# Mamba layer and mixture of experts on one core: scatters, a weight remainder and a norm re-ordered at the seam between scan and expert tiles

## The reference

```
x: 8 sequences x 512 tokens x 256 channels
x = layernorm(x + mamba(x))      # in_proj, conv of 4 taps, silu, softplus, a scan over time
                                 # with 16 states per channel, gate, out_proj, inner layernorm
x = layernorm(x + ffn(x))        # 8 experts, 4 of them per token by router logits:
    gate, up = x @ gate_up[e].T  # 256 -> 2 x 512
    act = (min(up,7)+1 ...) * silu-like(gate)
    out = act @ down[e].T        # 512 -> 256, weighted by a softmax over the 4 chosen
```

## Time and profile before

| | |
|---|---|
| median of 3 runs | 1254.55 us (1253.52 to 1254.76) |
| profiled execution | 1253.93 us, its span 1252.1 us |
| PE busy | 1144.7 us, 91% |
| DVE busy | 1043.4 us, 83% |
| ACT busy | 872.8 us, 70% |
| POOL busy | 759.1 us, 61% |
| mean granted TensorE clock | 0.959 |

### The profile page before, as it was taken

One profiled execution on the slowest core, in us unless ns is written; L12 is line 12 of the kernel. 1 busy time (PEld: TensorE's weight loads), 2 busy tenths in 40 slices (PEclk: granted clock), 3 DMA queues, 4 the chain that ended last, 5 costly groups with the idle time before them and its releaser, 6 DMA issues. The chain is left out here.

```text
span 1252.1 us, 17793 instructions
## 1 busy us (share of the span) xinstructions
PE 1144.7 (91%) x5150; PEld 795.0 (63%) x5150; DVE 1043.4 (83%) x1797; ACT 872.8 (70%) x1553; POOL 759.1 (61%) x535
## 2 busy tenths in 40 slices
PE   9889998999999997688999999999999999999950
PEld 4334353535343443257888888888888888888850
DVE  4999999999999999978876777777777777777744
ACT  4685959595969696625776777677777677677745
POOL 0456659888888887986764544454445544454453
PEclk9899999999999998898999999999999999999985
DMA  2643444646364645555796666656666566665638
GB/s 95 232 171 137 137 180 151 214 162 226 146 231 152 222 166 192 190 194 194 221 296 174 147 170 164 170 133 162 170 159 163 136 172 171 160 143 154 170 40 275
DMA packets 69263, 217.27 MB, mean 174 GB/s; under 512 B 7520, under 2 KB 43232, under 8 KB 56288
## 3 DMA queue, kind: packets, MB, share of 16 engines
q1 hardware_dynamic: 33888, 171.63, 37.4%
q0 software_dynamic: 26880, 36.72, 17.8%
q10 hardware_dynamic: 8448, 8.39, 2.0%
HBM read 165.55 MB, written 51.15 MB: 173 GB/s over the span
## 5 line engine op out<-in xcount | busy, mean ns | idle before, releaser
L1155 DVE TENSOR_TENSOR_SCAN state<-decay,p_bu 128x512 f32<-128x512 f32 x256 | 297.1, 1201 | 1.4 <-ACT decay L897 1.4
L697 PE MATMUL p_y<-read,small 128*128 128x512 f32 x512 | 252.6, 633 | 40.7 <-POOL read L1347 40.6
L1663 POOL DMA_INDIRECT total<-o_v,tok x136 | 252.8, 1859 | 37.5 <-issue 36.9
L697 PEld LDWEIGHTS p_y<-read,small 128*128 128x128 f32 x512 | 100.0, 201 | 178.6 <-issue 108.2
L1661 POOL TENSOR_TENSOR scrap<-neg_half 128x1 f32<-128x1 f32 x36 | 22.8, 633 | 271.6 <-ACT o_v L1579 259.2
L534 ACT ACTIVATE gate_v<-p_g,bias 128x512 f32<-128x512 f32 x144 | 98.7, 686 | 118.4 <-PE p_up L524 114.2
L542 DVE TENSOR_SCALAR up_v<-up_v 128x512 f32<-128x512 f32 x144 | 69.6, 483 | 129.7 <-ACT up_v L537 128.8
L897 ACT ACTIVATE decay<-dt,scan_rate 128x511 f32<-128x511 f32 x256 | 162.3, 709 | 10.6 <-DVE state L1155 10.0
L1347 POOL TENSOR_TENSOR read<-state,bc 128x1024 f32<-128x1024 f32 x64 | 127.6, 2000 | 27.8 <-DVE p_bu L1146 13.5
L555 ACT ACTIVATE ah<-a_v 128x512 fp32r<-128x512 f32 x144 | 91.5, 635 | 58.8 <-DVE a_v L548 58.8
L1389 POOL DMA_INDIRECT queues<-rows,index x112 | 115.5, 1031 | 26.8 <-issue 24.9
(11 more groups left out here) (247 smaller groups left out, 2984.6 us busy)
## 6 DMA issues: line engine op xcount, KB each, us to landing
bc<-bc_rows SPq DMA_DIRECT2D x32, 1024.0 KB, 4.8
first_raw<-in_w_experts SPq DMA_DIRECT2D x19, 1668.0 KB, 7.0
raw_w<-in_w_experts SPq DMA_DIRECT2D x18, 1668.0 KB, 7.1
first_wh<-bc_rows SPq DMA_DIRECT2D x16, 1024.0 KB, 4.7
first_wl<-bc_rows SPq DMA_DIRECT2D x16, 1024.0 KB, 5.0
first_rows<-queues SPq DMA_DIRECT2D x19, 544.0 KB, 3.6
xq<-queues SPq DMA_DIRECT2D x18, 544.0 KB, 3.7
queues<-pad SPq DMA_DIRECT2D x9, 544.0 KB, 6.2
```

Of the source, the lines that this page charges most:

```text
L697: mm = pe.matmul(p_y[h][:, :], ident[:, :], read[:, t % 4, h, :], start=False, stop=(t == SLOTS - 1))
L1155: dve.tensor_tensor_scan(state[t % 4][:, h, :], decay[(SLOTS * s.n + t) % AHEAD][:, h, :], p_bu[:, h * LEN:(h + 1) * LEN], 0.0, ALU.mult, ...
L1663: pool.indirect_dma_start(total, bass.IndirectOffsetOnAxis(ap=tokens_of(t)[:, a:a + 1], axis=0), output_of(t)[:, a, :], None, compute_op=A ...
```

## The change

It concerns the end of stage 1 and the first two tiles. (1) Sequence 5's seven scatters leave round 7: `SCATTERS` now applies only in rounds that also prepare a sequence, and all 16 stand in round 8, three ahead of the first power, one ahead of the second, three ahead of the third, nine behind. (2) Tile 0's three weight remainders move from behind the gate to ahead of it, with a wait for the reads that use the buffer they overwrite. (3) `last_norm1` works on each output bank by itself as it becomes full, so that there are three powers in place of two. (4) TensorE transposes tile 0's rows one slot later, sequence 7's rows between the chunks 2 and 3 of tile 0, and tile 1's rows behind the routing. (5) VectorE computes the remainder of tile 0's first product ahead of the last ranking, and the first remainder of tile 1's weights behind the last count.

```
@@ pe_stage1
                 if r.like == SEQS and t == 0:
                     transpose_rows(r, 0)
                     transpose_rows(r, 1)
+                if r.like == SEQS and t == 1:
                     pe.wait_ge(s_bu, halves_done(r.s, -1))
                     transpose_tile(pe, Seq(0, 0))
...
-                if r.d and t == 0 and r.like != SEQS:
+                if r.d and t == 0 and r.like < SEQS:
                     transpose_rows(r, 0)
                     transpose_rows(r, 1)
-                if r.last and t == 0:
-                    transpose_tile(pe, Seq(0, 1))
                 if r.d and t == 1:
                     route(r)
+                if r.last and t == 1:
+                    transpose_tile(pe, Seq(0, 1))
...
                         up_projection(pe, Seq(0, 0), i)
+                        if i == 2:
+                            transpose_rows(ROUNDS[-1], 0)
+                            transpose_rows(ROUNDS[-1], 1)
@@ dve_stage1
-        def last_moments(which, source):
+        def last_moments(k, which, some, source):
...
         def last_norm1(r):
-            banks = [full(dve, r, f"o{b}") for b in range(2)]
...
+            half = TT // 2
+            for b in range(2):
+                bank, done = full(dve, r, f"o{b}")
+                some = range(half * b, half * (b + 1))
+                last_moments(b, 0, some, lambda t: bank[:, t % 2 * D:(t % 2 + 1) * D])
+                for t in some:
+                    last = dve.scalar_tensor_tensor(z[:, t, :], bank[:, t % 2 * D:(t % 2 + 1) * D], last_neg[:, 0, t:t + 1],
+                                                    ln_g[:, :], ALU.add, ALU.mult)
+                last.then_inc(done, 1)
             for b in range(2):
                 bank, n = r.block(f"o{b}")
                 dve.wait_ge(bank_read[bank], n)
...
+                dve.wait_ge(s_last_rstd, b + 1)
+                for t in range(half * b, half * (b + 1)):
+                    last = dve.scalar_tensor_tensor(z[:, t, :], z[:, t, :], rstd[:, 0, t:t + 1], x[:, t, :], ALU.mult, ALU.add)
             last.then_inc(s_last_z, 1)
...
+                if r.like == SEQS and t == 2:
+                    dve.wait_ge(s_read, SLOTS * (SEQS - 1) + 4 * (RING - 1))
+                    for i in range(3):
+                        rest_of_weights(dve, early, i)
                 if r.c and t == 2:
                     gate(r)
-                if r.like == SEQS and t == 2:
-                    for i in range(3):
-                        rest_of_weights(dve, early, i)
...
-                    rest_of_weights(dve, second, 0)
+                if r.last and t == 2:
+                    rest_of_product(dve, early, 0)
...
                 if r.last and t == 3:
-                    rest_of_product(dve, early, 0)
...
                     rest_of_product(dve, early, 1)
+                    rest_of_weights(dve, second, 0)
                     rest_of_weights(dve, second, 1)
@@ pool_stage1
-        NEXT_TO_LAST = {8: (0, 1, 2), 10: (3,), 11: (4, 5), 12: (6,)}
...
-                scatters = NEXT_TO_LAST if r.like == SEQS - 1 else SCATTERS
-                if r.d and r.b and t in scatters:
-                    scatter(r.s.at(-2), scatters[t])
+                if r.d and r.a and t in SCATTERS:
+                    scatter(r.s.at(-2), SCATTERS[t])
...
                 if r.like == SEQS and t == 0:
-                    scatter(r.s.at(-3), range(7, 14))
-                    last_power(0)
-                    scatter(r.s.at(-3), range(14, TT * TOPK))
-                    last_power(1)
+                    scatter(r.s.at(-3), range(0, 3))
+                    last_power(0, 0, slice(0, TT // 2))
+                    scatter(r.s.at(-3), range(3, 4))
+                    last_power(1, 0, slice(TT // 2, TT))
+                    scatter(r.s.at(-3), range(4, 7))
+                    last_power(2, 1, slice(0, TT))
+                    scatter(r.s.at(-3), range(7, TT * TOPK))
```

More of the change, by code:

```diff
@@ L1173, in residual @@
             last.then_inc(s_residual, 1)
-        def last_moments(which, source):
-            for t in range(TT):
+        def last_moments(k, which, some, source):
+            for t in some:
                 last = dve.bn_stats(last_stats[:, t, :], source(t))
             last.then_inc(s_last_stats, 1)
-            dve.wait_ge(s_last_stats, which + 1)
-            for t in range(TT):
+            dve.wait_ge(s_last_stats, k + 1)
+            for t in some:
                 last = dve.bn_aggr(last_mv[:, which, t, :], last_stats[:, t, :])
@@ L1183, in last_moments @@
             last.then_inc(s_last_mv, 1)
[L1184 to L1187, removed]
-        def last_norm1(r):
-            banks = [full(dve, r, f"o{b}") for b in range(2)]
[L1193 to L1201, removed]
+            dve.wait_ge(s_last_mv, k + 1)
@@ new lines, in last_moments @@
+            cols = slice(some[0], some[-1] + 1)
+            dve.tensor_scalar(last_mv[:, which, cols, 1], last_mv[:, which, cols, 1], EPS, None, ALU.add)
+            dve.tensor_scalar(last_neg[:, which, cols], last_mv[:, which, cols, 0], -1.0, None, ALU.mult)\
+               .then_inc(s_last_eps, 1)
+            dve.wait_ge(s_last_eps, k + 1)
+        def last_norm1(r):
+            half = TT // 2
[3 more added lines that the diff above has]
+                last_moments(b, 0, some, lambda t: bank[:, t % 2 * D:(t % 2 + 1) * D])
+                for t in some:
+                    last = dve.scalar_tensor_tensor(z[:, t, :], bank[:, t % 2 * D:(t % 2 + 1) * D], last_neg[:, 0, t:t + 1],
+                                                    ln_g[:, :], ALU.add, ALU.mult)
+                last.then_inc(done, 1)
@@ L1204, in last_norm1 @@
                 dve.wait_ge(bank_read[bank], n)
-            dve.wait_ge(s_last_rstd, 1)
-            for t in range(TT):
-                last = dve.scalar_tensor_tensor(z[:, t, :], z[:, t, :], rstd[:, 0, t:t + 1], x[:, t, :], ALU.mult, ALU.add)
+                dve.wait_ge(s_last_rstd, b + 1)
+                for t in range(half * b, half * (b + 1)):
+                    last = dve.scalar_tensor_tensor(z[:, t, :], z[:, t, :], rstd[:, 0, t:t + 1], x[:, t, :], ALU.mult, ALU.add)
             last.then_inc(s_last_z, 1)
@@ L1213, in last_norm2 @@
             dve.wait_ge(s_last_z, 1)
-            last_moments(1, lambda t: z[:, t, :])
+            last_moments(2, 1, range(TT), lambda t: z[:, t, :])
             dve.tensor_copy(rows_of_seq(s)[:, :, COL_TOKEN].bitcast(I32), token[:, TT * s.n:TT * (s.n + 1)])
-            dve.wait_ge(s_last_rstd, 2)
+            dve.wait_ge(s_last_rstd, 3)
             for t in range(TT):
@@ L1362, in power, with last_power @@
                 .then_inc(s_rstd, 1)
-        def last_power(which):
-            pool.wait_ge(s_last_eps, which + 1)
-            pool.tensor_tensor(rstd[:, which, :], last_mv[:, which, :, 1], neg_half[:, :], ALU.pow).then_inc(s_last_rstd, 1)
+        def last_power(k, which, some):
+            pool.wait_ge(s_last_eps, k + 1)
+            pool.tensor_tensor(rstd[:, which, some], last_mv[:, which, some, 1], neg_half[:, some], ALU.pow)\
+                .then_inc(s_last_rstd, 1)
         def scale(r):
```

## The result

The changed kernel takes 1266.11 us (median of 4 executions, 1264.29 to 1266.57) against 1254.03 for the kernel before, measured beside it: ratio 1.0093, 95% interval 1.0079 to 1.0107. That is 12.1 us slower. The forecast was 7.6 slower, and its range ended at 1264.5. The profiled execution took 1266.57 us with a span of 1264.7, 12.6 above the span before. In both traces the last scan ends within 0.06 us of the same time, so rows of the two can be set side by side directly. Columns are as in the rows of before.

What follows compares the result with a forecast made beforehand. The prediction took GpSimd's chain of scatters and adds, reaching TensorE's tile loop through tile 4's token copy, as the bound. 1253.93 + 7.8 (chain) - 0.2 (tile 5) = 1261.5 us; range 1256.5 to 1264.5.

Steps and rivals of the forecast that it cites:

- The lock: Seam: VectorE's L498 and GpSimd's read 15 and offset exclude each other for whole instructions; gate at 551.8, 0.7 us later.
- the chain of scatters: GpSimd, seam: seven moved scatters at 1.27 us each, 8.9 us, stand in front of sequence 6.
- tile 4's token copy: VectorE, L578: waits 8 us or more for tile 2's adds, near 662; before, its wait measured 0.26 us.
- the half-clock start of tile 5: TensorE, tile 5: after 9 us without work it starts at half clock, costing 1.8 to 2.5 us.
- the vanished wait for rows: TensorE, behind tile 5's chunk 0: the 2.20 us wait for the next tile's rows goes.
- Rival A: Seam: no exclusion, reads slip through; gate at 548.4, chain +4.5 us, 1258.2 us; chance 0.14.
- B: Rival, GpSimd's chain: all 7.56 us of idle swallow the new work; 1252.9 us, no change; chance 0.10.
- C: Rival: GpSimd's chain does not bind, the seam's gain carries; faster, 1249.8 us; chance 0.08.
- D: Rival: slow scatters stay slow, or more collisions with tile 1's moved remainder; 1263.3 us; chance 0.08.
- the chain's shift: GpSimd: sequence 6's scatters start at 579.4 instead of 571.55, +7.8 us, passed on to tile 4's token copy.
- Nothing behind 571.55 can absorb it: GpSimd behind sequence 6's old start: the two idle spells, 2.23 and 2.93 us, are the chain's own; +7.8 us passes on.
- The -0.2 for tile 5: TensorE, tile 5: half-clock start (1.8 to 2.5 us) against the vanished 2.20 us wait for rows, net -0.2.

Runs made afterwards that it cites:

- the run with own tokens: The changed kernel with a token buffer of its own for tile 4, the wait for tile 2's adds moved in front of its read_output: 1.0037, median 1258.3 us.
- the gap filled: The changed kernel with six products of constants that nobody reads on TensorE between sequence 6's routing and project_out: 1.0067 of the kernel before, median 1263.13 us.
- the pads early: The changed kernel with SyncE's eight pad writes moved from tile 4's turn to tiles 2 and 3, four each: 1.0021 of the kernel before, median 1256.48 us.

## What the prediction had right, and the step that failed

**Right: the sign, the path and the place.** The lock (gate forecast at 551.8, 551.31 measured; from the scan 6.9 us, and 4.5 with the remainder behind it), the chain of scatters, the adds, tile 4's token copy with a wait of over 8 us, the half-clock start of tile 5 and the vanished wait for rows all stand in the trace as named. Rival A is refuted by the 7.08 us of L498. The Trainium skill (SBUF — State Buffer, Who interferes with whom) says that a VectorE instruction with two SBUF inputs contends with a GpSimd instruction that reads SBUF, over ports whose lock is exclusive; the 7.08, 2.90 and 2.97 us agree. B and C are refuted by the wait of 9.07 us.

On D the rows are with the prediction: the scatter at 580.88 took 1.93 us, beside tile 1's L498 (from 580.76), and the two ahead of it 1.00 and 1.06. The inference of the Trainium skill in the same section, that tensor_tensor doesn't hold up the writing of descriptors, does not agree with that row.

**The step that failed: the chain's shift, 7.8 forecast, 11.3 measured at sequence 6 and 12.0 at the token copy.** This put the time, 1266.11, above the range. It has two parts, and the first weighs more.

First, "Power 2 ends at 567.9; nine scatters at 1.27 follow, until 579.4". Power 2 ended at 569.99, because project_out ran at 1.2 GHz and the second bank was full at 562.8, not 560.4; the nine scatters took 12.65 us instead of 11.5. At full clock, in the run with own tokens, the shift of this step was 8.3; and with the gap filled the kernel was 8.6 us slower than before (1263.13 against 1254.58), inside the range. So the term left out is project_out's clock, some 3 us. I had named TensorE's clock as a way to be wrong, but for the scan's sums, not for the projection behind a gate that now leaves TensorE idle for 1.64 us. The lateness of 3.2 us with which VectorE came to tile 4's tokens is the same spell: at full clock it was there at 110.1 to 110.8 us from the scan, as before.

Second, "Nothing behind 571.55 can absorb it: the two idle spells there are the chain's own". They do not stay as they were. The first, the 2.23 us before 597.90, is a pause for which no trace names a cause; it grew to 5.08, which took the shift from 10.0 us to 12.9, but the issues around it made up for that. The second is a landing, and what else is under way decides how long it takes. The chain's shift was 11.7 us when tile 1's last add had been issued, 15.7 when the wait for its landing ended, and 12.0 when tile 2's adds had landed. It is luck that the 4.0 of the one landing and the -3.7 of the next nearly cancel here: with the gap filled 8.3 at sequence 6 became 10.6 at tile 2's landing, with the pads early 9.9 became 5.5. The shift moved tile 1's adds under SyncE's pads, and nearly the same shift with the pads elsewhere (sequence 6 at 37.0 us from the scan instead of 38.5) cost 1.85 us of waiting at the copy instead of 9.07. Pads are not the only transfers beside which a landing came late: with the pads moved in the kernel before, the wait for tile 2's adds was 7.52 us beside a load of weights, though no run moved that load by itself. The Trainium skill (DMA: Bandwidth & Descriptors, Issuing engines are not separate DMA queues) has transfers of all engines run on the same DMA engines and interleave; the waits of 6.97 and 3.77 us agree with that.

The -0.2 for tile 5 came out between 0 and +0.6: shift at the copy 12.0, in the span 12.6, in the medians 12.1. Tile 1's up products came 0.8 us later instead of 1 to 1.5 earlier (584.37 against 583.61), under the cold spell.

## What to carry to other kernels

When work is pushed down an in-order queue, follow it to the next landing that someone waits for, and look up what another queue sends at that time: here a shift was not handed on one to one, since it slid transfers under somebody else's bulk, or out from under it. Before moving work, look for the wait that is just at its limit (0.26 us here) and give it slack (a buffer more, a wait put where the buffer is really overwritten, padding sent when the queues are free); here moving the padding gained 3.5 us in the kernel before, where the change gained nothing. And when a reordering opens idle time ahead of a long run of products, price these at the lower clock as well.

## What was unexpected of the hardware

Moving the buffers by 16 bytes per partition, with no other difference, made the tile loop 2.2 us shorter (and so in the traces of all five kernels with that shift). TensorE is busy throughout in both, at a granted clock of 1.00; most of its gate and up products are shorter by some ns in the mean, the group below most, while some down products are longer. Groups by line of the kernel before and of the shifted one, 730 to 1150 us:

```profile
L524 PE MATMUL p_up<-xh,first_wh 128*128 128x512 f32 x96 | 38.0, 396 | 0.0
```

```profile
L525 PE MATMUL p_up<-xh,first_wh 128*128 128x512 f32 x96 | 37.3, 389 | 0.0
```

Why is open. Also open is GpSimd's pause between the first and the second scatter of sequence 7, 2.23 us before and 5.08 in the changed kernel, 2.09 to 6.60 over all traces, for which none names a cause. And the half-clock spell of project_out came in the profiled executions of the changed kernel and of three variants, but not in that of the run with own tokens, with the same code and the same idle time ahead.
